# The last stage of a fused attention and feed-forward kernel: one product for the rotation's second half, floor and power of the norms for two chunks at once

## What is computed

```python
def l2norm(t):
    return t / jnp.maximum(jnp.linalg.norm(t, axis=-1, keepdims=True), 1e-12)

def rotate_half(x):
    x1, x2 = jnp.split(x, 2, -1)
    return jnp.concatenate([-x2, x1], -1)

def attn_layer(x, Wqkv, qs, ksc, Wo):
    qkv = x @ Wqkv
    q, k, v = jnp.split(qkv, 3, -1)          # 16 heads of 64
    q = l2norm(q) * qs
    k = l2norm(k) * ksc
    q = q * cos * scale + rotate_half(q) * sin * scale
    k = k * cos * inv + rotate_half(k) * sin * inv
    out = local_attention(q, k, v)           # windows of 32, each with the one before
    return out @ Wo

for i in range(6):
    x = attn_layer(shift_tokens(x), Wqkv[i], q_scale[i], k_scale[i], Wo[i]) + x
    x = ffn_layer(shift_tokens(x), ln_g[i], ln_b[i], W1[i], b1[i], W2[i], b2[i]) + x
```

## Time and profile before

| | |
|---|---|
| median of 3 runs | 2322.89 us |
| lowest and highest | 2321.42 and 2332.89 us |
| the profiled execution | 2328.08 us |
| its span, from the first to the last instruction | 2326.2 us |
| mean granted clock of TensorE | 0.919 |
| busy: TensorE, VectorE, ScalarE, GpSimd | 80%, 74%, 55%, 39% of the span |

### The profile page before, as it was taken

The page is one execution under the profiler, slowest core; times in us unless marked ns, Lnnn a source line. Parts: engine busy times, 40 slices in busy tenths (PEclk is TensorE's granted clock), DMA queues, the critical chain, the costliest instruction groups (busy, mean ns, idle before and its releaser), DMA issues. The chain is left out here.

```text
span 2326.2 us, 52273 instructions
## 1 busy us (share of the span) xinstructions
PE 1867.0 (80%) x18512; PEld 924.7 (40%) x18512; DVE 1716.5 (74%) x3041; ACT 1279.5 (55%) x1850; POOL 906.5 (39%) x913
## 2 busy tenths in 40 slices
PE   5745888888888888888846887887888888788786
PEld 3531222222222222222223654654655555555564
DVE  4744677767777777777648988878878887887893
ACT  4411665656666666666635655645546555555553
POOL 0012111111111111111028858648657666675670
PEclk9955898989999999999958998999999999999998
DMA  1002223232222232222004323323323333232330
GB/s 34 1 24 61 46 56 61 56 59 55 59 55 59 55 59 55 59 55 57 2 30 119 92 85 92 87 85 92 94 87 92 86 93 92 68 111 75 84 84 10
DMA packets 88745, 152.83 MB, mean 66 GB/s; under 512 B 16819, under 2 KB 51669, under 8 KB 84693
## 3 DMA queue, kind: packets, MB, share of 16 engines
q1 hardware_dynamic: 86421, 149.04, 26.2%
q10 hardware_dynamic: 2112, 0.94, 0.2%
HBM read 98.03 MB, written 51.12 MB: 64 GB/s over the span
## 5 line engine op out<-in xcount | busy, mean ns | idle before, releaser
L899 DVE TENSOR_REDUCE ENM<-PM 128x1 f32<-128x512 f32 x1024 | 658.4, 685 | 257.2 <-PE PM L722 248.8
L819 ACT ACTIVATE EPT<-PA 128x1024 f32<-128x1024 f32 x512 | 512.4, 1021 | 220.2 <-PE PA L734 137.6
L722 PE MATMUL PM<-EKX,EQX 48*128 48x512 bf16 x1024 | 356.3, 402 | 104.3 <-DVE ENM L899 84.0
L1279 POOL TENSOR_TENSOR DQR<-DR 128x512 f32<-128x512 f32 x192 | 245.4, 1278 | 289.0 <-DVE DR L1569 289.0
L1281 POOL TENSOR_TENSOR DRN<-DRN,DHALF 128x8 f32<-128x8 f32 x192 | 354.8, 1848 | 8.4
L642 POOL CAST ENMP<-ENM 128x16 bf16<-128x16 f32 x64 | 12.6, 196 | 786.2 <-DVE ENM L899 786.2
L744 PE MATMUL PV<-EPT,EVP 128*32 128x512 f32 x2048 | 286.7, 633 | 0.8 <-ACT EPT L819 0.7
L734 PE MATMUL PA<-EQX,EKX 51*128 51x512 bf16 x1024 | 254.8, 397 | 28.4 <-DMA EQX<-EROWS 15.9
L722 PEld LDWEIGHTS PM<-EKX,EQX 48*128 48x128 bf16 x1024 | 85.8, 95 | 482.1 <-DVE ENM L899 392.7
L1325 PE MATMUL PM<-DWQKV,DXS 128*128 128x512 f32 x384 | 218.0, 651 | 47.3 <-ACT XNT L1526 29.2
L1487 ACT ACTIVATE DRAW<-PM 128x512 f32<-128x512 f32 x192 | 114.7, 598 | 143.4 <-PE PM L1325 106.4
(11 more groups left out here) (208 smaller groups left out, 2960.9 us busy)
## 6 DMA issues: line engine op xcount, KB each, us to landing
DV<-d_vpark SPq DMA_DIRECT2D x192, 256.0 KB, 5.0
d_vpark<-DVT SPq DMA_DIRECT2D x48, 512.0 KB, 2.6
e_park<-EPARTS SPq DMA_DIRECT2D x64, 192.0 KB, 2.9
EQX<-e_park SPq DMA_DIRECT2D x32, 384.0 KB, 5.5
EKX<-e_park SPq DMA_DIRECT2D x32, 384.0 KB, 9.2
DWQKV<-in_WqkvR SPq DMA_DIRECT2D x6, 1536.0 KB, 9.5
e_park<-EPARTS SPq DMA_DIRECT2D x64, 128.0 KB, 2.7
e_park<-EPARTS SPq DMA_DIRECT2D x64, 64.0 KB, 2.1
```

The lines of the kernel that those rows point to most:

```text
L722: pe.matmul(PM[:, r, :], lhsT=QX[64 * r:64 * r + KQ, b, hp, t * 128:(t + 1) * 128], rhs=KX[64 * r:64 * r + KQ, b, hp, :], start=True, stop ...
L819: s_.activation(PT[:, kt, pair * 2 * S:(pair + 1) * 2 * S], PA[:, 2 * pair:2 * pair + 2, :].rearrange("p a b -> p (a b)"), ACT.Exp, scale= ...
L899: v.tensor_reduce(NM[:, g % 2, t, j, 0:1], PM[:, r, :], AX.X, ALU.max, negate=True).then_inc(maxed, 1)
L1279: g.tensor_tensor(qr, r1, r2, ALU.add).then_inc(roped.sem if queries else joined.sem, 1)
```

## The change

The two instructions of lines 1568 and 1569 become one of 512 columns, which reads the halves of each head in swapped order (a step of -1 over the halves). `SS` has 16 columns, and is filled by the reductions of two chunks; the floor is done once behind chunks 1 and 3, over 16 columns. GpSimd takes the power of 16 values behind the adds of chunks 1 and 3. Both key chunks are scaled behind the power of chunk 3, one after the other. `floored` and `rooted` count pairs of chunks.

```diff
-        HALF = m.sb("DHALF", [128, 8])
+        HALF = m.sb("DHALF", [128, 16])
-        SS, RN = m.sb("DSS", [128, 2, 8]), m.sb("DRN", [128, 2, 32])
+        SS, RN = m.sb("DSS", [128, 2, 16]), m.sb("DRN", [128, 2, 32])
...
                         g.tensor_tensor(qr, r1, r2, ALU.add).then_inc(roped.sem if queries else joined.sem, 1)
-                        pool.wait_ge(floored.sem, floored.at(layer, k))
-                        g.tensor_tensor(rn, rn, HALF[:, 0:8], ALU.pow).then_inc(rooted.sem, 1)
-                        if not queries:
-                            pool.wait_ge(joined.sem, joined.at(layer, 2 * n[0] + n[1] - 2))
-                            pool.wait_ge(rooted.sem, rooted.at(layer, k))
-                            g.tensor_tensor(qr.rearrange("p (h e) -> p h e", h=8), qr.rearrange("p (h e) -> p h e", h=8),
-                                            bc(rn, 2, [128, 8, DL]), ALU.mult).then_inc(roped.sem, 1)
+                        if n[1] % 2:
+                            rn = RN[:, n[0] % 2, 8 * n[1] - 8:8 * n[1] + 8]
+                            pool.wait_ge(floored.sem, floored.at(layer, k // 2))
+                            g.tensor_tensor(rn, rn, HALF[:, :], ALU.pow).then_inc(rooted.sem, 1)
+                        if n[1] == 3:
+                            for c in range(2):
+                                qr = QR[:, (k - 1 + c) % 4, :].rearrange("p (h e) -> p h e", h=8)
+                                pool.wait_ge(joined.sem, joined.at(layer, 2 * n[0] + c))
+                                pool.wait_ge(rooted.sem, rooted.at(layer, k // 2))
+                                g.tensor_tensor(qr, qr, bc(rn[:, 8 * c:8 * c + 8], 2, [128, 8, DL]), ALU.mult).then_inc(roped.sem, 1)
...
                         v.tensor_tensor(r1, x, bc(tab[:, 0], 1, [128, 8, DL]), ALU.mult).then_inc(step, 1)
-                        v.tensor_tensor(r2[:, :, 0:32], x[:, :, 32:64], bc(tab[:, 1, 0:32], 1, [128, 8, 32]), ALU.mult).then_inc(step, 1)
-                        v.tensor_tensor(r2[:, :, 32:64], x[:, :, 0:32], bc(tab[:, 1, 32:64], 1, [128, 8, 32]), ALU.mult).then_inc(rotated.sem, 1)
+                        halves = lambda y: y.rearrange("p h (s e) -> p h s e", s=2)
+                        v.tensor_tensor(halves(r2), halves(x)[:, :, ::-1, :], bc(tab[:, 1].rearrange("p (s e) -> p s e", s=2), 1, [128, 8, 2, 32]),
+                                        ALU.mult).then_inc(rotated.sem, 1)
                         wait(squared, k)
-                        v.tensor_reduce(SS[:, k % 2, :], SQ[:, k % 2, :].rearrange("p (h e) -> p h e", h=8), AX.X, ALU.add).then_inc(summed.sem, 1)
-                        wait(summed, k)
-                        v.tensor_scalar(RN[:, n[0] % 2, 8 * c:8 * c + 8], SS[:, k % 2, :], 1e-24, None, ALU.max).then_inc(floored.sem, 1)
+                        v.tensor_reduce(SS[:, k // 2 % 2, 8 * (c % 2):8 * (c % 2) + 8], SQ[:, k % 2, :].rearrange("p (h e) -> p h e", h=8), AX.X, ALU.add).then_inc(summed.sem, 1)
+                        if c % 2:
+                            wait(summed, k)
+                            v.tensor_scalar(RN[:, n[0] % 2, 8 * c - 8:8 * c + 8], SS[:, k // 2 % 2, :], 1e-24, None, ALU.max).then_inc(floored.sem, 1)
                     elif name == "score":
...
-                        wait(rooted, 4 * n + 1)
+                        wait(rooted, 2 * n)
```

More of the change, by code:

```diff
@@ L1152, in stage_d @@
         summed, rotated = ev("summed", 4 * NT, 2), ev("rotated", 4 * NT, 2)
-        floored = ev("floored", 4 * NT)
-        joined, rooted = ev("joined", 2 * NT), ev("rooted", 4 * NT)
+        floored = ev("floored", 2 * NT)
+        joined, rooted = ev("joined", 2 * NT), ev("rooted", 2 * NT)
         roped = ev("roped", 4 * NT, 2)
@@ L1273, in piece @@
                         r1, r2 = (x[:, k % 2, :] for x in (R1, R2))
-                        rn = RN[:, n[0] % 2, 8 * n[1]:8 * n[1] + 8]
                         qr = QR[:, k % 4, :]
```

## The result

The changed kernel takes 2372.28 us (median of 4 runs, 2365.12 to 2373.95), the kernel before 2326.23 us (4 runs): a ratio of 1.019, 95% interval 1.0154 to 1.0227. The forecast was 2361 with a range of 2318 to 2380, so direction and size came out, with 46 us in place of 38; the time also lies within the narrower 2346 to 2376.

A forecast was written before the change was run, and what follows sets the result against it. VectorE was taken to set the pace in steady steps, partly held by GpSimd at shared ports. Per layer 3.6 + 0.25 + 0.1 + 3.0 - 0.7 = 6.25; six layers add 38 to 2322.9: 2361 us, range 2318 to 2380.

The forecast's parts named there:

- the exclusion at the ports: Full-tile GpSimd instructions and VectorE instructions with two SBUF inputs, or the floor, exclude each other, first come first served.
- (1): Rotation's second half on VectorE: the merged product costs 0.60 instead of 0.68 us per chunk, 15 us of VectorE.
- (3): GpSimd's powers: 192 of 8 become 96 of 16, each 2.95 us, ending 1.3 us later.
- My rival for that case: The power hardly grows from 1.65 us: 2321 us; chance 0.14, shared with a power that grows by half.
- (5): End of steady steps: both late scalings meet the subtraction and delay the next product, +1.0 per step, +3.0 per layer.
- (6): Steps 0 and 1 of a layer: no score covers floor, power and two scalings; together +3.6 us per layer.
- (7): Steps with the layer norm's power, and step 3: step 2 +0.25, step 7 -0.7, step 3 +0.1 us.
- (4): GpSimd's order in a steady step: chunk 1's add holds its floor, about +0.5; the subtraction still starts at 15.2.
- the saved work is simply saved: Rival for the last stage: holds don't move to the next instruction, -46 us, 2277 us; chance 0.13.
- my picture of holds that always pass on: Where a removed floor stood in line behind GpSimd, the next product is held at the ports in its place.

The follow-up runs named there:

- the first run: Kernel before with only the second-half products merged into one of 512 columns: 2325.29 us, ratio 0.9984.
- The run with the other wait: Changed kernel, with VectorE's chunks 0 and 1 waiting for the key chunks' adds instead of their scalings: 2333.77 us, ratio 1.0032.

## Why the prediction was right, and where it was not

**What bounds the kernel, and the exclusion at the ports.** Right. The held instructions of the changed kernel came with the forecast durations: floor of chunk 1 (0.74), the product after the scalings (1.52). The wait in front of step 1 is 4.03 where I had said some 3.

**(1) One product.** Its price was right (0.69 in the mean, 0.60 from start to start). That it gains little alone is shown by the first run: 0.7 us per layer in the table, where 15 us of VectorE's time would be 2.5.

**(3) The power.** Right: 2.92 measured, 2.95 forecast by the slope of two durations. The second of these, the unheld 1.65, stands in none of the rows ahead; it is in the last section below. The Trainium skill ("GPSIMD Engine Reference", section "Instruction dispatch") gives about 2.5 cycles per element as the least that two-input work takes. The power takes far more: 2.91 for 16 columns against 1.65 for 8. The run with the power of 8 shows that this length decides the sign. My rival for that case was 2321, the run gave 2311.

**(5) Steps 4 to 6.** Three times +1.0 forecast; the table has +0.9, +1.5 and +1.8. This is the term that was mis-sized: 3.0 against 4.2 per layer. Step 4 came as written in layers 2 to 6 (layer 3, timeline of both engines):

```profile
1684.28 1.22 DVE L1588 TENSOR_TENSOR DP<-DP,DMAX 128x1024 f32<-128x1024 f32 x1
1684.38 3.02 POOL L1288 TENSOR_TENSOR DQR<-DQR,DRN 128x512 f32<-128x512 f32 x2
1686.44 1.52 DVE L1569 TENSOR_TENSOR DR<-DRAW,DTAB 128x512 f32<-128x512 f32 x1 [0.94 <-POOL DQR L1288]
```

The subtraction begins 15.2 us into the step, the first scaling 0.1 behind it, and the next step starts 18.2 after this one. What is above 18.2 in steps 5 and 6 comes from TensorE. In step 5 it now waits 2.93 us for the mixed values, which chunk 1's held instructions delay (1.55 before). Behind that wait its granted clock is lower, between the levels of 1.2 and 2.4 GHz in the mean. The changed kernel's stretch and its rows, from the busy-time view and TensorE's timeline:

```profile
1693.00:1699.00 6.00, 5.92 (x32) 4.50 (x32) 5.55 (x10) 2.90 (x5) 4.04 (x3) 0.72 0.74 167
```

```profile
1693.08 1.71 PE L144 MATMUL PA<-IDENT,DP 128*128 128x128 f32 x8 [2.93 <-DVE DP L1599]
1694.58 1.92 PE L1327 MATMUL PM<-DWQKV,DXS 128*128 128x512 f32 x2
```

The kernel before, at the same place of its step (busy-time view, then the timeline):

```profile
1674.00:1680.00 6.00, 6.00 (x162) 4.76 (x160) 5.90 (x13) 2.80 (x5) 5.86 (x5) 1.00 0.69 198
```

```profile
1673.68 1.25 PE L144 MATMUL PA<-IDENT,DP 128*128 128x128 f32 x8 [1.55 <-DVE DP L1595]
1674.77 1.02 PE L1325 MATMUL PM<-DWQKV,DXS 128*128 128x512 f32 x2
```

The projection takes 1.92 instead of 1.02, and VectorE waits twice, before chunk 3 and before the score:

```profile
1697.24 0.69 DVE L1569 TENSOR_TENSOR DR<-DRAW,DTAB 128x512 f32<-128x512 f32 x1 [0.41 <-ACT DRAW L1489]
...
1701.00 1.23 DVE L1583 TENSOR_TENSOR DP<-PA,DRN 128x1024 f32<-128x1024 f32 x1 [0.89 <-PE PA L1355]
```

Chunk 3's floor ends 0.5 us later than in step 4, and so does the step (18.67). The same step of the first layer shows that the wait alone doesn't cost this: there TensorE waits 3.08 us, its clock stays full, and the step takes 18.03.

```profile
1319.00:1325.00 6.00, 5.42 (x104) 4.29 (x107) 5.96 (x10) 2.80 (x5) 4.60 (x3) 1.00 0.73 174
```

```profile
1319.58 1.26 PE L144 MATMUL PA<-IDENT,DP 128*128 128x128 f32 x8 [3.08 <-DVE DP L1599]
1320.67 1.02 PE L1327 MATMUL PM<-DWQKV,DXS 128*128 128x512 f32 x2
```

At the end of step 6 it is another wait: TensorE stands 2.96 us for nothing that the profile shows, its projection is slow again, and chunk 0 of step 7 waits for it (both engines; then the busy-time view of the stretch, and of the same place in layer 4):

```profile
1721.26 1.54 PE L144 MATMUL PA<-IDENT,DP 128*128 128x128 f32 x6 [2.96 <-issue]
1722.59 1.79 PE L1327 MATMUL PM<-DWQKV,DXS 128*128 128x512 f32 x2
1725.22 0.69 DVE L1569 TENSOR_TENSOR DR<-DRAW,DTAB 128x512 f32<-128x512 f32 x1 [2.87 <-ACT DRAW L1489]
```

```profile
1721.00:1725.00 4.00, 3.74 (x13) 2.54 (x14) 1.32 (x2) 1.69 (x4) 3.12 (x3) 0.61 0.00 0
1910.00:1914.00 4.00, 4.00 (x20) 2.59 (x21) 2.26 (x4) 3.23 (x7) 2.77 (x3) 1.00 0.00 0
```

In layer 4 TensorE stood 3.23 us there, the clock is full behind it, the projection takes 1.02 and the step 18.19; in layers 2, 3 and 5 the projection is slow and the step takes 19.95, 19.29 and 19.96. The kernel before has one such step 6 in layers 2 to 5 (layer 5, 18.43). So in both cases with a full clock the step takes the forecast 18.2 or less, and the surplus goes with the lower clock; that rests on these two cases, not on a run made for it. Why it fell in some layers and not in others, and what TensorE stood for in step 6, stays open. Of the stage's 192 projections of queries and keys, 27 take over 1.3 us for both passes, against 15 before.

**(6) Steps 0 and 1.** +3.6 forecast, +3.65 measured (17.30 + 18.90 against 13.44 + 19.11). Step 0 has +3.9, as forecast, and step 1 gives 0.2 back. The run with the other wait took 7.1 us out here, which I had given as 2.5: the step that failed there was to price the ports as high as the semaphore.

**(7) Steps 2, 7 and 3.** +0.25 and -0.7 forecast, +0.24 and -0.96 measured. The layer norm's power came as forecast, 8.1 into the step by its effective start:

```profile
1626.19 1.01 POOL L1291 TENSOR_TENSOR RSTD<-STD,DHALF 128x4 f32<-128x4 f32 x1
1627.23 1.36 DVE L1620 TENSOR_SCALAR XN<-PV,MV,RSTD 128x128 f32<-128x128 f32 x4 [2.49 <-POOL RSTD L1291]
```

Step 3 has +0.8 where I had 0.1; the rest of this is not explained.

**The sum.** 6.25 per layer forecast, 8.0 in the table for layers 2 to 5. The layers differ: 3.8, 11.0, 7.4, 4.1, 9.5, and 10.7 in the last with the end of the program. I took all six alike, so that the total comes as near as 46 against 38 is in part luck: the first layer's small loss hides some of what the lower clock adds in the others.

**The queries.** (4) set their +0.5 in front of L1595 against small gains in the same step, and the sum came out near zero. In the changed kernel that held (the subtraction begins at 15.2 wherever the clock is full), since chunk 2 has no floor. The run with the queries alone shows that this was not a property of the queries' pairing: with chunk 2's floor back, the same long power costs 1.2 us per steady step.

**The rivals.** That the saved work is simply saved fell for the change as a whole. But its core, that a removed floor is worth its busy time, was nearer than my picture of holds that always pass on: some 50 us for 192 floors whose group books 95 in the run with the one product.

## What to carry to other kernels

Joining two small instructions into one makes sense where the fixed part is the larger; here the power had 0.35 us fixed and 0.16 per column, so the pair saved 0.4 of 3.3 us, and its second half was ready 1.3 us later than by a power of its own, the first half later still. Before moving work on one engine, list who meets whom at a shared resource just before and just after: the same instruction costs 0.17 or 0.75, a product 0.68 or 1.53, by which of the two began first. And ask of each held instruction what stands behind it: if that reads elsewhere, the hold is a true cost, and taking the held instruction away is worth more than its unheld time. A gain found in one arrangement need not hold in the next: moving both scalings behind chunk 3 was free with the floors and cost 1.9 us in step 5 without them.

## What the runs showed of the hardware that I had not expected

GpSimd's power doesn't keep VectorE's products out for its length, as an add or a scaling of 512 columns does. Two meetings in the steady step of the kernel before (timeline of both engines), the first with the product ahead, the second with the power ahead:

```profile
1674.13 0.68 DVE L1567 TENSOR_TENSOR DR<-DRAW,DTAB 128x512 f32<-128x512 f32 x1
1674.23 2.11 POOL L1281 TENSOR_TENSOR DRN<-DRN,DHALF 128x8 f32<-128x8 f32 x1
...
1677.53 1.65 POOL L1281 TENSOR_TENSOR DRN<-DRN,DHALF 128x8 f32<-128x8 f32 x1
1677.62 0.69 DVE L1567 TENSOR_TENSOR DR<-DRAW,DTAB 128x512 f32<-128x512 f32 x1
```

The power behind a product takes 2.11 instead of 1.65; the product behind a power is not held at all (0.69). It is so in the whole stage of the kernel before: of 281 products that begin within a power, over 0.3 us before its end, none takes over 0.69 us, and the 5 floors that do take 0.17; the 89 powers that begin within a product take 2.07 in the mean, the others 1.66. The Trainium skill ("SBUF — State Buffer", section "Who interferes with whom"), speaking of VectorE's two-port modes, gives the pair of ports to the first "for the whole instruction"; for the power these rows differ.

A step of -1 over the halves costs a VectorE product nothing (0.69 for 512 columns, as the first product of the same size). A bias column makes ScalarE's square of 512 columns 0.09 us longer (726 against 635 ns in the run without floors).
